# A state-space and routing kernel: the row statistics of the first norm move from VectorE to ScalarE for three of four sequences

## What is computed

```python
# a state-space layer over the context, gated by the normalised x
u  = silu(causal_conv4(ctx @ in_proj.T) + conv_b)
dt_low, Bm, Cm = split(u @ x_proj.T)           # 32, 16 and 16 rows
dt = softplus(dt_low @ dt_proj.T + dt_b)
for t in tokens:                               # 1024 channels x 16 states
    state = state * exp(dt[t] * A) + (dt[t] * u[t]) * Bm[t]
    y[t]  = sum_n(state * Cm[t])
y  = (y + D * u) * silu(layernorm(x))          # the first norm
x2 = x + tanh(g1) * y
# an expert layer on layernorm(x2): router softmax, top 256 tokens of each expert
out = x2 + tanh(g2) * moe(layernorm(x2))
```

## Time and profile before

| | |
|---|---|
| median of 3 runs | 2131.61 us (2131.18 to 2132.29) |
| profiled execution, its own time | 2129.65 us |
| its span in the trace | 2127.5 us |
| prologue, to the first input of slot 0 | 0 to 65.49 us |
| first half | 65.49 to about 323.3 us |
| last scan | ends near 1902 us |
| busy | DVE 1931.3 us, POOL 1736.6 us, PE 1654.1 us, ACT 1405.6 us |

### The profile page before, as it was taken

How to read it: one execution, slowest core, us unless ns; L and a number is a source line. 1 busy time by engine, 2 the same in 40 slices (tenths; PEclk the granted TensorE clock), 3 DMA queues, 4 the chain that set the end, 5 groups by cost and what they waited for, 6 DMA issues and landing times.

```text
span 2127.5 us, 23357 instructions
## 1 busy us (share of the span) xinstructions
PE 1654.1 (78%) x7564; PEld 1082.5 (51%) x7564; DVE 1931.3 (91%) x2055; ACT 1405.6 (66%) x2115; POOL 1736.6 (82%) x758
## 2 busy tenths in 40 slices
PE   7456666678888888888878988889888778778790
PEld 2234444454555555555555555555555555556340
DVE  7988989999999899999999999999999999982667
ACT  3455756787788768786888777876888687742000
POOL 0488989998999999998999999999999999980000
PEclk9678888889999999999999988999999889886995
DMA  9600214133844465345735473537524553355088
GB/s 368 251 26 16 85 62 183 31 125 101 307 130 145 139 228 185 118 155 181 246 115 178 127 283 111 177 111 267 170 89 149 198 198 114 126 186 196 6 311 354
DMA packets 139001, 348.19 MB, mean 164 GB/s; under 512 B 15234, under 2 KB 17794, under 8 KB 129666
## 3 DMA queue, kind: packets, MB, share of 16 engines
q1 hardware_dynamic: 133698, 327.83, 44.4%
q10 hardware_dynamic: 5184, 18.88, 2.3%
HBM read 301.04 MB, written 45.61 MB: 163 GB/s over the span
## 4 chain that ended last, share of the span: by engine, by line
POOL 25%; PE 25%; DVE 19%; issue 15%; ACT 10%; DMA 4%; SPq 0%; DVEq 0%; POOLq 0%; ACTq 0%
POOL states L1366 15%; DVE states L1105 11%; POOL states L1354 8%; PE pY L599 7%; PE pM L693 5%; PE pA L567 4%; ACT pDec L852 4%; DVE states L1090 2%; PE pA L576 2%; DVE u L1080 2%; PE pDec L705 2%; ACT L836 1%; DMA bbc<-bc_scratch 1%; POOL dtub L1345 1%; PE pY L595 1%
## 5 line engine op out<-in xcount | busy, mean ns | idle before, releaser
L1366 POOL TENSOR_TENSOR states<-states,cbc 128x2048 f32<-128x2048 f32 x256 | 1160.5, 4536 | 32.5 <-DVE states L1105 21.8
L852 ACT ACTIVATE pDec<-steps,an 128x512 f32<-128x512 f32 x1024 | 685.1, 687 | 412.8 <-DVE states L1105 408.4
L599 PE MATMUL pY<-con,states 128*128 128x128 f32 x4096 | 587.0, 306 | 185.1 <-POOL states L1366 184.9
L599 PEld LDWEIGHTS pY<-con,states 128*128 128x128 f32 x4096 | 541.3, 160 | 303.3 <-POOL states L1366 242.1
L1105 DVE TENSOR_TENSOR_SCAN states<-pDec,carry,states 128x512 f32<-128x512 f32 x512 | 625.9, 1265 | 25.5 <-ACT pDec L852 24.9
L1105 DVE TENSOR_TENSOR_SCAN states<-pDec,states 128x512 f32<-128x512 f32 x512 | 594.8, 1204 | 37.8 <-ACT pDec L852 37.6
L1354 POOL TENSOR_TENSOR states<-dtub,bbc 128x1024 f32<-128x1024 f32 x192 | 454.3, 2366 | 63.4 <-PE pY L599 50.7
L693 PE MATMUL pM<-wk,xfT 128*128 128x512 f32 x832 | 424.6, 626 | 2.3 <-DMA wk<-in_expert_w 2.3
L1090 DVE TENSOR_TENSOR states<-pU,bbc 128x1024 f32<-128x1024 f32 x320 | 384.9, 1203 | 5.0 <-DMA bbc<-bc_scratch 3.5
L567 PE MATMUL pA<-ctx_sb,winb 128*128 128x512 f32 x448 | 228.4, 657 | 62.7 <-issue 30.1
L693 PEld LDWEIGHTS pM<-wk,xfT 128*128 128x128 f32 x832 | 148.3, 204 | 83.8 <-issue 82.2
(11 more groups left out here) (206 smaller groups left out, 1421.5 us busy)
## 6 DMA issues: line engine op xcount, KB each, us to landing
wk<-in_expert_w SPq DMA_DIRECT2D x416, 256.0 KB, 4.3
bbc<-bc_scratch SPq DMA_DIRECT2D x32, 1024.0 KB, 7.3
cbc<-bc_scratch SPq DMA_DIRECT2D x32, 1024.0 KB, 9.4
sz<-in_x SPq DMA_DIRECT2D x34, 512.0 KB, 6.0
xt<-in_x SPq DMA_DIRECT2D x15, 1024.0 KB, 5.6
winb<-in_winT SPq DMA_DIRECT2D x58, 256.0 KB, 2.6
x_scratch<-xt SPq DMA_DIRECT2D x14, 1024.0 KB, 6.0
xr<-x_scratch SPq DMA_DIRECT2D x28, 512.0 KB, 4.0
```

Source lines behind the costliest of these rows:

```text
L599: mm = pe.matmul(pY[:, eT(t)], states[g % NST][:, i, eT(t)], ident, start=False, stop=(q == QG - 1 and i == QN - 1 and t == TT - 1), is_tr ...
L852: nc.scalar.activation(pDec[bank_of(h, k)][:], dt[e % 2], ACT.Exp, scale=an[:, k:k + 1]).then_inc(s_dec, 1)
L1366: nc.gpsimd.tensor_tensor(st, st, cbc[:, QW * q:QW * (q + 1), :], ALU.mult).then_inc(s_hc, 1)
```

## The change

Only the first sequence's statistics stay on VectorE: four groups instead of sixteen, from tiles in `xt`, `xr`, `wk` and `pairs[3]`. The other 24 tiles are read during half 0 by ScalarE, in 12 pairs that take turns in `xr` and in the first two tiles of `wk`. A pair is four tasks, `row_task`, in four following slots from slot 8 on, and then one slot without: copy with sum, copy with sum and the negated means, square with sum, square with sum. SyncE loads a pair when the pair before the last has been read. The variance and bias of the three sequences move from slots 8 to 10 to slots 68 to 70, which is slots 4 to 6 of half 1. B and C are loaded without a wait for statistics. The context of half 0 comes in four transfers, one for each quarter of the contraction, behind the first weights, and TensorE waits for each quarter. ScalarE's and VectorE's first block of the convolution now stands ahead of the small constants.

```diff
+NROWS = (B - 1) * E // 2
+ROW_SLOT = [8 + 5 * (i // 4) + i % 4 for i in range(4 * NROWS)]
+LN1_SLOT = ROW_SLOT[-1] + 2
...
-        stage = [x for t in (bbc, *pairs, cbc, sz) for x in tiles_of(t)]
-        stage += tiles_of(xt) + [xr[0][:], xr[1][:]] + tiles_of(wk)
+        places = [[xr[0][:], xr[1][:]], tiles_of(wk)[:2]]
+        stage = [*tiles_of(xt), *places[0], *places[1], *tiles_of(pairs[3])]
+        stage += [x for i in range(NROWS) for x in places[i % 2]]
...
+            def load_rows(i):
+                if i < 2:
+                    sp.wait_ge(s_ln1, 2 * (i + 2))
+                else:
+                    sp.wait_ge(s_rows, 5 * (i - 1))
+                load_stage(E // 2 + i)
...
             def side(h, g):
+                if h == 0 and g == 0:
+                    load_rows(0)
+                    load_rows(1)
+                for i, k in at(ROW_SLOT, g, h):
+                    if k == 0 and i % 4 == 3 and i // 4 + 2 < NROWS:
+                        load_rows(i // 4 + 2)
...
-            load_ctx(0)
             sp.dma_start(win_first[0], winT[0]).then_inc(s_wf[0], 16)
+            for part in range(KC):
+                sp.dma_start(ctx_sb[:, part, :], ctxT[0, :, part, :]).then_inc(s_cf[part] if part < KC - 1 else s_ctx, 16)
...
-            sp.wait_ge(s_ln1, 2 * STAGED_B)
-            for q in range(3):
-                load_b(0, q)
-            sp.wait_ge(s_ln1, 2 * STAGED_C)
-            for q in range(2):
-                load_c(0, q)
+            load_b(0, 0)
+            load_b(0, 1)
+            load_c(0, 0)
+            load_b(0, 2)
+            load_c(0, 1)
...
+            def row_task(i):
+                pair, task = divmod(i, 4)
+                t = task % 2
+                k = 2 * pair + t
+                tile = places[pair % 2][t]
+                b, e = divmod(E + k, E)
+                if task == 0:
+                    act.wait_ge(s_stage[E // 2 + pair], 16 * 2)
+                if i:
+                    act.wait_ge(s_rows, 5 * pair + (0, 1, 3, 4)[task])
+                if task < 2:
+                    nc.scalar.activation(unread[:], tile, ACT.Copy, accum_out=sums1[:, t:t + 1]).then_inc(s_rows, 1)
+                if task == 1:
+                    act.wait_ge(s_rows, 5 * pair + 2)
+                    nc.scalar.activation(nm1[:, b, e - 1:e + 1], sums1, ACT.Copy, scale=-1.0 / D).then_inc(s_rows, 1)
+                if task >= 2:
+                    nc.scalar.activation(unread[:], tile, ACT.Square, bias=nm1[:, b, e:e + 1],
+                                         accum_out=sq1[:, b, e:e + 1]).then_inc(s_rows, 1)
...
             act.wait_ge(s_w, 16 * NW)
+            xin_ready(0, 0, pIn[0])
             nc.scalar.activation(al, al, ACT.Exp).then_inc(s_c, 1)
...
-            LATE_STATS = {g: i for g, i in zip((1, 2, 3, 5, 6), range(11, 2 * E))}
-            for j in range(E):
-                for i in range(HALO):
-                    conv(0, j, i, pIn[j])
-                if j:
-                    ln1_stats(j - 1)
...
+            conv_first(1)
+            ln1_stats(0)
+            for j in range(2, 5):
+                conv_first(j)
+            ln1_stats(1)
+            for j in range(5, E):
+                conv_first(j)
+            ln1_stats(2)
+            ln1_stats(3)
+            ln1_variance(0)
```

93 lines of the change are left out of this document (50 added, 43 removed).

## The result

The changed kernel takes 2117.28 us (median of 4 runs, 2116.27 to 2119.94); the kernel before takes 2131.95 beside it (4 runs, 2131.18 to 2133.0). The ratio is 0.9933, with a 95% interval of 0.9916 to 0.995: 14.7 us faster, of the 18.5 that were forecast. The time lies 4.3 us above the forecast and inside its range.

What follows compares the result with a forecast made beforehand. VectorE alone was taken to set the pace in slots 0 to 10, with no engine full behind them. The terms -17.8 - 12.7 + 8 + 4 = -18.5 us gave 2113 us from the runs' median, range 2099 to 2127.

Steps and rivals of the forecast that it cites:

- The prologue: Up to VectorE's first input of slot 0: fewer statistics groups and an earlier, shorter store gain 17.8 us, bounds 14 and 19.
- TensorE's last block is done at 10 + 7 x 3.43 = 34.0: Prologue: TensorE starts near 4 us, ends its first block near 10, and its last at 34.0.
- silu 0.64, matmuls 1.98, copy 0.69: Prologue, behind the last convolution at 37.2 us: these and small gaps put the store of B and C at 40.6.
- Slots 0 to 10: Start of half 0: VectorE loses five statistics groups and two small operations; 12.7 us gained, at least 9, at most 18.
- GpSimd then comes last: Slots 0 to 10: GpSimd's operations, laid behind the loads, end last, at 43.8 us behind slot 0.
- ScalarE: forecast +8: Slots 8 to 66: row tasks add some 60 us of ScalarE work behind 122 us; 8 us lost, from nothing to 15.
- ScalarE becomes the pace: Rival, half 0 behind 122 us: ScalarE's work stretches 201 us to 220, +19 to +25, giving 2124 to 2131; chance 0.19.
- Slower: Rival, half 0: every task lengthens its slot because a decay behind it misses its scan; 2166 us, chance 0.06.
- The tasks hide: Rival, half 0: ScalarE's gaps take the row tasks and loads come in time; 2100 us, as low as 2090; chance 0.2.
- Half 1: Slots 68 to 70: the variance and bias come again where VectorE works 214 of 225 us; 4 us lost, 0 to 5.4.
- the last rival: Prologue, the change doesn't do what it says: store of B and C lands as late as now; 2121 to 2124, chance 0.03.

Runs made afterwards that it cites:

- E7: The changed kernel again without an edit, on another chip: 2123.33 us, ratio 0.9958 to the kernel before.
- E2: The changed kernel with all four of VectorE's statistics groups behind the last convolution, none between: one run of 2119.27 us.
- E8: The changed kernel with the second block's weights issued ahead of the small constants: one run of 2122.22 us.
- E1: The changed kernel with the context of half 0 in one transfer again, still behind the first weights: one run of 2121.07 us.
- E4: The changed kernel with the first two pairs of rows loaded in slot 3, behind B's and C's last quarters and the first gates: 2114.76 us, ratio 0.9909.
- E3: The changed kernel with ScalarE's row tasks reading only 8 of 1024 features: 2113.57 us, ratio 0.9908 to the kernel before.
- E10: The changed kernel with the edits of E2, E4 and E8, row tasks out of softplus, silu and gate slots but allowed in gates' copy slots: 2110.3 us.
- E5: The changed kernel with row tasks kept out of softplus, silu and gate slots and five gate-copy slots, the last in slot 75: 2115.85 us, ratio 0.9922.

## Why the prediction was right, and where it was off

**The prologue: forecast -17.8, measured -14.5.** The mechanism was right: two statistics groups ahead of the last convolution instead of six, and a store ahead of the staged rows. The store of B and C was issued at 44.00 us instead of the 40.6 that were forecast, it landed 0.9 us sooner than the sum had it (1.61 against 2.5), and the first quarter of B took 0.8 more (5.4 us from the store's end to its use, against 4.62). That gives slot 0 at 51.0 instead of 47.7.
(In E7's trace it is 51.9, a gain of 13.6, just outside the 14 to 19 that were named.) The 3.4 us of the store's issue come from two terms, both TensorE's. The first is "TensorE's last block is done at 10 + 7 x 3.43 = 34.0": it was done at 36.1. TensorE started at 5.22, not near 4, its second block began at 11.75 after a wait for weights that the sum didn't have, and a block took 3.48 us. So the last convolution ended at 39.4, 2.2 us late. The second is the tail, "silu 0.64, matmuls 1.98, copy 0.69". It took the last two matmuls of the projection from the earlier trace rows, since the fourteen ahead of them were hidden behind VectorE there. They aren't now: all sixteen run behind the last block, 7.08 us from 36.11 on. ScalarE's last silu was done at 40.08, two matmuls more would be 42.1, and `xpr` was copied at 43.29. The 1.98 us was a price at the granted clock of 0.50; at 1.00, where a matmul takes 0.44 us, two would have ended near 41.0. So the fourteen cost 2.3 us, of which the higher clock hid 1.1. That TensorE is the limit is shown by E2, where VectorE's way to the last convolution is 5.4 us lighter and slot 0 moves by 0.67, and by E8, where TensorE's wait for weights goes and slot 0 moves by 1.24.

The Trainium skill (DMA: Bandwidth & Descriptors, section Bandwidth) advises at least 1 MiB for each DMA, and the prediction took from it that the start could stay near 6.5 us. That advice is about the rate of a transfer. For the start of the first consumer the traces of this case speak against it: TensorE starts at 6.43 us with one piece (E1) and at 5.22 with quarters.

**Slots 0 to 10: forecast -12.7, measured -8.8 (to slot 11).** GpSimd's fifth `times_c` ended 44.3 us behind slot 0; 43.8 was forecast, and the waits for B's quarters came nearly where they were laid. Up to there 12.1 us were gained, so this sum was right. The step that failed is "GpSimd then comes last": TensorE did. Its projection and sums end 5.8 us behind the fifth `times_c` instead of 2.4, and these 3.4 us are the difference between 12.1 and 8.8. Part of the reason lies in the loads. The four row tiles had been counted against B's last quarter alone, and the gates stand behind them too, with ScalarE, its decays, VectorE's convolution and the turned gate behind one another. With the rows behind both (E4) the stretch is 13.7 us shorter than before the change, and GpSimd's fifth `times_c` and the projection both end sooner. But TensorE is last there too: VectorE waits 4.27 us for the sums.

**ScalarE: forecast +8, measured +10.5.** The size was near and the reason holds. The work was priced too high: 60 us in this stretch, where ScalarE's busy time rose by 42.6 (125.9 to 168.5). 41 tasks stand in it, and the 49.8 us by which all 48 with their means raise ScalarE's busy time are 1.04 each, not the 1.28 to 1.33 of the sum, since rows that follow each other overlap by about 0.1 us (a square at 92.58 lasts 1.15, the read behind it starts at 93.63). So ScalarE was never at 187 of 201 us. E3 shows that full length carries 7.8 of the 10.5 us, and E10 that the places carry 7: largely the same microseconds, since neither a short task in a bad slot nor a long one in a quiet slot delays decays much. "ScalarE becomes the pace" wanted a loss wherever the work stands, but in E5 37 full tasks, by which ScalarE's busy time in this stretch is 36 us longer than before the change (161.8 against 125.9), cost it 1.3 us. "Slower", 0.55 us or more passed on by every task, falls by the same number. "The tasks hide" is what E5 shows for other places, not what the changed kernel does.

**Half 1: forecast +4, measured +1.3** for halves 1 to 7 together, and +4.5 in E7's trace. The variance took 4.12 us, more than the 2.15 of the earlier trace rows, and the bias 0.20 instead of 3.25; their sum of 4.3 us was near the 5.4 by luck. Both ended 0.04 us behind GpSimd's current operation, as the two rows of before did. The variance had begun 0.46 us into a product, the bias 0.16 us ahead of an input's end, so how long each lasts depends on where in that operation it happens to start. By the Trainium skill (SBUF — State Buffer, section Who interferes with whom) such a wait can last one whole instruction of GpSimd, and the 4.12 us row agrees. The prediction tied it to two SBUF inputs; the variance has one in its row, and waited. In slot 1 the row at 57.88 lasted 0.14 us, because GpSimd was itself waiting for B, so the wait that the prediction allowed there didn't occur.

**The store** landed in 1.61 us, sooner than the 2 to 4 that were named, so the last rival falls. **The end** lost 2.0 us, for which the sum had no term; it lies within what this stretch varies in the runs here (217.2 to 223.4), and its cause stays open.

**The sum** of the stretches is -9.4 us against -18.5, and the medians give -14.7. The rest is in the two profiled executions, one 2.7 us above its median and one 2.3 below. In E7's set the medians give -8.7, which is 2123.33: still in the range, 10 us above the forecast. Half 1 was to begin near 300 us and begins at 310.6 (E7: 310.5). Three of the four terms fell short in the trace, and the end, for which the sum had no term, went the same way; their signs were right. That the first set came within 4.3 us of the forecast is therefore in part luck.

## What to carry to other kernels

When a chain of waits ends on one engine, the other engines' work just ahead of its end is hidden and not free: take off the first, and all of the hidden work (here sixteen matmuls, not two) stands there. When bulk loads are moved off one transfer's way, list every later small load on the queue that they are now ahead of, and who is queued behind the engine that waits for it. And extra work on an engine with slack in short pieces is priced by where it stands: the same tasks cost half 0 some 10 us when eight of the 41 share a slot with table loads, and 1 to 3 us when none does. When one engine is relieved, look at what each of the others must still finish in program order before the next step: here it was TensorE's projection ahead of its sums.
